# The closing stage of an attention and mixture-of-experts layer: rows normalised, turned and projected one chunk ahead of the experts' sum

## The reference

```python
xn = _layernorm(x, axis=-1)                       # x: (4, 1024, 256)
s = _L0_attn_ref(xn, ...)                         # differential attention, 8 heads
g = _silu(_L0_ffn_ref(xn, ...))                   # 8 experts, the best 2 of each token, weighted
return x + s * g

# the end of _L0_attn_ref: out is the attention's result
o = out.reshape(b, nh, s, nh, dv // nh)
o = o32 * jax.lax.rsqrt(jnp.mean(o32 * o32, axis=-1, keepdims=True) + EPS)
o = o.reshape(b, nh, s, dv) * (1.0 - L_INIT)
return jnp.einsum('bsd,od->bso', o.transpose(0, 2, 1, 3).reshape(b, s, nh * dv), wo)

# the end of _L0_ffn_ref: scores holds two weights for each token
out = jnp.einsum("te,eth->th", scores, expert_out)
```

## Time and profile before

| | |
|---|---|
| median of 3 runs | 1115.05 us (1113.02 to 1116.56) |
| the profiled execution: its time, its span | 1113.86 us, 1112.0 us |
| closing stage in the span | 995 to 1112 us |
| busy in 993 to 1112 us | PE 60.48, DVE 83.57, ACT 62.71, POOL 69.68 us |
| granted TensorE clock in 993 to 1112 us | 0.70 of full speed |

### The profile page before, as it was taken

The page is one execution under the profiler, slowest core; times in us unless marked ns, Lnnn a source line. Parts: engine busy times, 40 slices in busy tenths (PEclk is TensorE's granted clock), DMA queues, the critical chain, the costliest instruction groups (busy, mean ns, idle before and its releaser), DMA issues. The chain is left out here.

```text
span 1112.0 us, 25771 instructions
## 1 busy us (share of the span) xinstructions
PE 941.5 (85%) x6626; PEld 659.5 (59%) x6627; DVE 938.0 (84%) x1873; ACT 776.8 (70%) x1982; POOL 221.7 (20%) x427
## 2 busy tenths in 40 slices
PE   5999858989889998988999898858999999962665
PEld 4787645666666666666666666644555555532544
DVE  6778688999999999999999999935777777754987
ACT  3554438999999999999999999942333333325663
POOL 2000001222222232222322232210000000017771
PEclk9999987999999999999999999988999999996677
DMA  7999986676786767757575665402222222223553
GB/s 258 377 366 370 328 318 137 172 183 149 172 199 165 175 157 187 184 128 165 120 159 130 139 151 128 95 15 66 80 84 77 85 80 80 80 94 96 174 182 107
DMA packets 92410, 178.11 MB, mean 160 GB/s; under 512 B 11744, under 2 KB 50144, under 8 KB 91360
## 3 DMA queue, kind: packets, MB, share of 16 engines
q1 hardware_dynamic: 74336, 147.38, 49.1%
q0 software_dynamic: 7680, 20.98, 6.5%
q10 hardware_dynamic: 10368, 9.44, 2.5%
HBM read 108.56 MB, written 69.21 MB: 160 GB/s over the span
## 5 line engine op out<-in xcount | busy, mean ns | idle before, releaser
L1050 DVE TENSOR_REDUCE nmax<-bank 128x1 f32<-128x1024 f32 (+3 forms) x256 | 260.4, 1017 | 4.0 <-PE bank L882 4.0
L983 ACT ACTIVATE Pr_long<-bank,nmax 128x1024 f32<-128x1024 f32 (+3 forms) x256 | 252.0, 984 | 12.2 <-DVE nmax L1050 12.1
L1010 ACT COPY AT<-bank 128x512 f32<-128x512 f32 (+3 forms) x384 | 177.0, 493 | 4.4 <-PE bank L921 2.5
L880 PE MATMUL bank<-Ks_first,Qs_first 128*128 128x512 f32 (+3 forms) x384 | 124.1, 413 | 31.1 <-ACT Pr_short L997 19.8
L1242 PE MATMUL bank<-gu_sb,xsT 128*128 x288 | 140.7, 612 | 4.8 <-DVE hid L1359 0.5
L997 ACT ACTIVATE Pr_short<-bank,nmax 128x128 f32<-128x128 f32 (+3 forms) x256 | 138.3, 540 | 8.9 <-DVE nmax L1068 1.6
L921 PE MATMUL bank<-ident,Pr_long 128*128 128x128 f32 x832 | 127.9, 281 | 18.1 <-DVE Pr_long L1100 18.1
L1100 DVE SCALAR_TENSOR_TENSOR Pr_long<-Pr_long,coef 128x1024 f32<-128x1024 f32 (+3 forms) x128 | 137.6, 1075 | 0.0
L880 PE MATMUL bank<-Ks_second,Qs_second 128*128 128x512 f32 (+3 forms) x384 | 119.4, 400 | 18.7 <-ACT Pr_short L997 18.4
L882 PE MATMUL bank<-maskb,identb 128*128 128x128 bf16 x512 | 118.1, 233 | 0.0
L921 PEld LDWEIGHTS bank<-ident,Pr_long 128*128 128x128 f32 x832 | 90.8, 143 | 31.7 <-issue 27.6
(11 more groups left out here) (147 smaller groups left out, 1647.0 us busy)
## 6 DMA issues: line engine op xcount, KB each, us to landing
q_parts<-PARTS SPq DMA_DIRECT2D x32, 512.0 KB, 5.9
k_parts<-PARTS SPq DMA_DIRECT2D x32, 512.0 KB, 5.9
Qs_first<-q_parts SPq DMA_DIRECT2D x64, 256.0 KB, 6.2
Ks_first<-k_parts SPq DMA_DIRECT2D x64, 256.0 KB, 7.1
Qs_second<-q_parts SPq DMA_DIRECT2D x64, 256.0 KB, 5.9
Ks_second<-k_parts SPq DMA_DIRECT2D x64, 256.0 KB, 6.7
xs_dram<-zeros SPq DMA_DIRECT2D x8, 1152.0 KB, 8.4
xs<-xs_dram SPq DMA_DIRECT2D x72, 128.0 KB, 2.0
```

The lines of the kernel that those rows point to most:

```text
L880: nc.tensor.matmul(at[:, c0:c1], Qs[head][:, m, q * P:(q + 1) * P], Ks[head][:, m, c0:c1], start=True, stop=(c1 < N))
L983: nc.scalar.activation(long_probs(p)[:, m, 0:N], long_slot[m][:, 0:N], ACT.Exp, bias=nmax[:, 4 * p + m:4 * p + m + 1], scale=1.0, accum_ou ...
L1010: nc.scalar.copy(AT[u % 6][:, 0:w], tb[u % BANKS][:, 0:w]).then_inc(unit_out, 1)
L1050: nc.vector.tensor_reduce(nmax[:, 4 * p + m:4 * p + m + 1], long_slot[m][:, 0:N], AX.X, ALU.max, negate=True).then_inc(long_maxed, 1)
```

## The change

Nothing is computed differently, and no buffer or semaphore is added. `curves` becomes `root_curve` and `silu_curve`; `normalise` becomes `mean_squares`, `both_experts` and `scaled_rows`. A body for chunk c now holds, on DVE, `mean_squares(c+1)`, `both_experts(c)`, `scaled_rows(c+1)`, `finish(c)`, and on ACT `squares(c+1)`, `first_expert(c)`, `root_curve(c+1)`, `silu_curve(c)`, `turned_out(c+1)`. PE, POOL and SP have the same instructions in the same order.

```diff
-                    def curves(b, h):
+                    def root_curve(b, h):
                         act.wait_ge(on_ready, credited(b, 4, 2 * h - 1))
                         act.wait_ge(ms_ready, credited(b, 2, h))
                         nc.scalar.activation(root[:], square_sum[:], ACT.Sqrt, scale=1.0 / half_gain ** 2
                                              ).then_inc(root_ready, 1)
+
+                    def silu_curve(b, h):
                         act.wait_ge(res_ready, credited(b, 2, h - 2))
                         act.wait_ge(ff_ready, credited(b, 2, h))
...
                     squares(0, 0)
-                    first_expert(0, 0)
-                    curves(0, 0)
+                    root_curve(0, 0)
+                    turned_out(0, 0)
                     def batch(b, more):
                         for h in range(2):
                             after = (b + (h + 1) // 2, (h + 1) % 2)
                             if more or h == 0:
                                 squares(*after)
-                            turned_out(b, h)
+                            first_expert(b, h)
                             if more or h == 0:
-                                first_expert(*after)
-                                curves(*after)
+                                root_curve(*after)
+                            silu_curve(b, h)
+                            if more or h == 0:
+                                turned_out(*after)
...
-                    run_chunks(dve, normalise, finish)
+                    def batch(b, more):
+                        for h in range(2):
+                            after = (b + (h + 1) // 2, (h + 1) % 2)
+                            if more or h == 0:
+                                mean_squares(*after)
+                            both_experts(b, h)
+                            if more or h == 0:
+                                scaled_rows(*after)
+                            finish(b, h)
+
+                    mean_squares(0, 0)
+                    scaled_rows(0, 0)
+                    with dve.Fori(0, B - 1) as b:
+                        batch(b, True)
+                    batch(B - 1, False)
```

More of the change, by code:

```diff
@@ L1515, in outputs @@
                         "p j t d -> p j (t d)")
[L1517 to L1528, removed]
                 @block.tensor
@@ L1627, in _, with mean_squares @@
                         dve.sem_inc(s, 2)
-                    def normalise(b, h):
+                    def mean_squares(b, h):
                         nc.vector.tensor_copy(d1x[:], d1_all[:, bass.ds(b * NH, NH), h * CT:(h + 1) * CT]
@@ L1648, in normalise, with both_experts @@
                             op0=ALU.mult, op1=ALU.add).then_inc(ms_ready, 1)
+                    def both_experts(b, h):
                         dve.wait_ge(ff_half, credited(b, 2, h))
@@ L1656, in normalise, with scaled_rows @@
                         last.then_inc(ff_ready, 1)
+                    def scaled_rows(b, h):
                         dve.wait_ge(root_ready, credited(b, 2, h))
```

## The result

The changed kernel takes 1107.61 us (median of 4 runs, 1106.94 to 1108.87) against 1115.39 us (4 runs): a ratio of 0.9935, 95% interval 0.9919 to 0.9952, or 7.8 us less. Measured again beside three experiments it was 1105.56 against 1113.71, 0.9922 (0.9908 to 0.9936). The forecast was 7.9 us less and 1107.0. The profiled execution took 1106.94 us, its span is 1105.1.

A forecast was written before the change was run, and what follows sets the result against it. POOL's gather issue was taken as the pace, with a serial 20.55 us end behind it. The end's 8.77 us less 0.9 for POOL's pace saves 7.9: 1106.0 or 1107.2 us, forecast 1107.0, range 1104.6 to 1110.4.

The forecast's parts named there:

- The end: Serial work from the last ACT weighting to the span's end: 11.78 us against 20.55, shorter by 8.77 us.
- The start: Chunk 0's squares, root, scaling, transposes and copies, 11.5 us, move into the 12.1 us wait; cost 0, at most 0.5.
- The count of table loads: ACT's closing stage: three loads added over the stage, two dropped (chunk 0's and the last tanh's).
- The bodies: Per-chunk work, next chunk's squares now behind the copies: cost 0, hidden behind POOL's pace of 11.9 us.
- the margin that was named: Spare time before the next additions: 0.1 us in bodies with the table load, 1.4 us in the others.
- the ring: Waits over ACT, DVE, PE between chunks' additions: 11.8 us with table load, 10.4 without; rival that it sets pace, chance 0.04.
- POOL's pace: Gather issues stretched beside DVE's finish: one more long interval, 11.98 for 11.06, costs 0.9 us; bounds 0 to 1.57.
- The base: Time the saving is subtracted from: profiled execution 1113.86 us, or median 1115.05, giving 1106.0 or 1107.2.
- The sum: Whole kernel: 8.77 - 0.9 = 7.9 us saved, 1106.0 us from the profiled 1113.86.

## Why the prediction was right

**The end: right, and shown.** Forecast 11.78 us from the last weighting, measured 11.84; each step came within 0.1. The last projection ended 2.2 us ahead of the products (1096.95 against 1099.11), where 1.7 were forecast. Undoing this part alone gave the kernel before again (0.9996).

**The start: cost nothing, as forecast.** It fits in the wait ahead of chunk 0, with 0.51 us left (forecast 0.6). What it is worth the prediction did not say, beyond that POOL would not notice some tenths; with chunk 0's additions about 8 us late POOL waited 2.60 us, and the run was 4.8 us slower. The count of table loads was off by one, without effect: chunk 0's was not dropped, it stands in the start (ACT's loads in the stage are 18 against 16).

**The bodies: right, with the margin that was named.** I left 0.1 us in the body with the table load, and in one of the two ACT indeed has no gap and DVE goes from sums to additions without a wait (1057.52 to 1059.28). In the other (the load at 1030.31) ACT waited 0.86 us for the gather. Taking the squares out of the ring changed nothing measurable, though the load stayed. Making it 2.1 us longer cost what the ring's sum says. The table load took 1.28 with at most 0.02 behind it in all places of the changed kernel; the 1.38 us of drain that the Trainium skill gives in "ScalarE: Activation LUTs", "What ACT_TABLE_LOAD costs", are not seen here.

**POOL's pace: mechanism right, size 0.5 for 0.9, and in part by luck.** One more distance became long, as one more finish beside the gathers has it. It grew by 1.27 (12.29 for 11.02) and not by 0.92, which I had read from the starts of the weightings. That the sum still came out smaller is something I had not foreseen: of the later distances two became shorter (11.69 and 11.74 for 12.28 and 12.23) and one longer (12.22 for 11.83). The trace shows what sets them apart. In the long ones an issue begins 0.54 us into the first step of the finish and takes 1.50 (1064.81 against 1064.27), and the copy of `yslot` takes 0.72; in the short ones it begins 0.88 us into the step and takes 1.17 (1053.10 against 1052.22), and the copy takes 0.54. What makes the two alternate was not tried.

That DVE operations with both inputs in SBUF are the cause was an inference from one row, and is now borne out: leaving two such operations out, and doing them with one input in PSUM, both brought the distances to 11.0 to 11.4, and operations of full length with one input in PSUM do not stretch an issue either. On this the Trainium skill, "SBUF — State Buffer", "Who interferes with whom", says two things. That such an operation keeps off a GpSimd instruction that reads SBUF agrees with the copy of `yslot`, 0.72 beside it and 0.20 without. Its inference that the building of descriptors is not held up by a `tensor_tensor` does not agree: beside the addition, a `tensor_tensor` with both inputs in SBUF, a gather's issue took 1.52 in place of 0.95.

```profile
1020.25 1.23 DVE L1684 TENSOR_TENSOR xr<-ft,xr 128x1024 f32<-128x1024 f32 x1
...
1020.80 1.52 POOL L1507 DMA_INDIRECT yg<-ys_dram,yslot  x1 [0.81 <-POOL yw L1501]
```

**The base.** The sum was made from 1113.86 and gave 1106.0; the profiled execution after took 1106.94, of which 1.28 is a later start of the stage that the change can't touch. The medians differ by 7.8 us, against 7.9; inside the stage of the profiled executions it is 8.2. That the medians hit the sum to 0.1 is luck, since the times of one kernel scatter by 2 to 5 us.

## What to carry to other kernels

Where a stage is paced by one queue, look at what stands behind that queue's last delivery and does not need it: moving that ahead pays once, and in full as long as the bodies stay hidden behind the queue. Count the ring through the engines that the new order closes, not the engines' busy time; here it had an estimated 0.1 us left in two bodies, and 2 us more of work on a half-idle engine took back two thirds of the gain. When the last piece is cut into smaller ones, what counts is the queue of pieces behind the first wait, and not the last piece.

## What was not expected of the hardware

A gather's issue on POOL and a small copy on POOL both get longer beside a DVE operation with two SBUF inputs (0.95 to 1.50, 0.20 to 0.72), and neither does beside one with one input in PSUM (0.95, 0.20); over the stage this is 4 us. Three kernels that used a further PSUM bank for the finish had gaps of up to 11 us on ACT, DVE and TensorE, and times that scatter by 7 to 11 us where the others scatter by 2 to 5. In the first of them the waits in the gaps end with increments of TensorE's semaphores, recorded 11 and 14 us behind the end of the work that they report; the cause is open.
